# Three PSUM slots and three one-hot buffers in the two attention passes of a graph network, in place of two each

## What is computed

```
h       = (x @ W).reshape(N, heads, outc)
alpha_s = (h * a_s).sum(-1);  alpha_d = (h * a_d).sum(-1)
e     = leaky_relu(alpha_s[src] + alpha_d[dst], 0.2)
m     = segment_max(e, dst);  p = exp(e - m[dst])
z     = segment_sum(p, dst);  alpha = p / (z[dst] + 1e-16)
out   = segment_sum(h[src] * alpha[:, :, None], dst)
```

## Time and profile before

| | us |
|---|---|
| median of 3 runs | 25891.91 |
| lowest and highest | 25857.63, 25914.94 |
| profiled execution: span | 25860.5 |
| PE busy | 20502.8 |
| DVE busy | 19538.6 |
| POOL busy | 14550.5 |
| ACT busy | 12983.1 |
| first attention pass, first to last start of its fetch matmuls | 861.1 to 3825.1 |
| second attention pass, likewise | 4282.1 to 8128.3 |

### The profile page before, as it was taken

One profiled execution on the slowest core, in us unless ns is written; L12 is line 12 of the kernel. 1 busy time (PEld: TensorE's weight loads), 2 busy tenths in 40 slices (PEclk: granted clock), 3 DMA queues, 4 the chain that ended last, 5 costly groups with the idle time before them and its releaser, 6 DMA issues. The chain is left out here.

```text
span 25860.5 us, 355868 instructions
## 1 busy us (share of the span) xinstructions
PE 20502.8 (79%) x110397; PEld 18592.4 (72%) x110397; DVE 19538.6 (76%) x36629; ACT 12983.1 (50%) x15054; POOL 14550.5 (56%) x14357
## 2 busy tenths in 40 slices
PE   0688874888885799978999638888888889489996
PEld 0577763888785688867888538888888888278885
DVE  4699995777776699987999626666666667499997
ACT  0455551222221466644666316666666667266664
POOL 1555545555554555554555467666776675355555
PEclk9999996999997899998999859999999999599998
DMA  5222221111111111111111111111111111522221
GB/s 91 59 71 71 71 69 22 37 40 37 40 37 31 37 40 40 40 32 40 36 35 35 23 14 19 19 19 18 19 18 19 19 19 15 147 67 71 71 71 50
DMA packets 1347467, 1106.63 MB, mean 43 GB/s; under 512 B 937658, under 2 KB 1197972, under 8 KB 1320180
## 3 DMA queue, kind: packets, MB, share of 16 engines
q1 hardware_dynamic: 673364, 571.63, 8.0%
q0 software_dynamic: 545440, 167.01, 7.8%
q10 hardware_dynamic: 127872, 358.35, 3.8%
HBM read 646.52 MB, written 448.94 MB: 42 GB/s over the span
## 5 line engine op out<-in xcount | busy, mean ns | idle before, releaser
L973 PE MATMUL gat_e_found<-gat_e_parts,gat_e_lowhot 128*128 128x400 f32 x27776 | 5657.0, 363 | 1270.4 <-DVE gat_e_rows L937 974.6
L973 PEld LDWEIGHTS gat_e_found<-gat_e_parts,gat_e_lowhot 128*128 128x128 f32 x27776 | 5301.1, 199 | 1625.9 <-DVE gat_e_rows L937 1225.8
L1091 POOL DMA_INDIRECT gat_e_rows<-att_t,gat_e_index x3968 | 3767.0, 949 | 3046.1 <-issue 1509.8
L1966 PEld LDWEIGHTS rgcn_e_found<-rgcn_e_parts,rgcn_e_lowhot 128*128 128x128 f32 x23808 | 4295.3, 188 | 667.9 <-DVE rgcn_e_picked L1811 455.5
L760 POOL DMA_INDIRECT rgcn_e_rows<-rel_t,rgcn_e_index x3472 | 3284.4, 946 | 2506.3 <-DMA rgcn_e_rows<-rel_t,rgcn_e_index 1137.9
L1966 PE MATMUL rgcn_e_found<-rgcn_e_parts,rgcn_e_lowhot 128*128 128x400 f32 x23808 | 4543.8, 348 | 173.4 <-DVE rgcn_e_picked L1811 133.8
L2527 PE MATMUL sheaf_e_bysrc<-sheaf_e_exacthot,sheaf_e_masked 128*128 128x392 f32 x19840 | 4217.8, 370 | 423.7 <-ACT sheaf_e_exacthot L2630 365.4
L2258 POOL DMA_INDIRECT sheaf_e_rows<-sheaf_t,sheaf_e_index x3224 | 3386.3, 1050 | 1695.5 <-issue 886.8
L2527 PEld LDWEIGHTS sheaf_e_bysrc<-sheaf_e_exacthot,sheaf_e_masked 128*128 128x128 f32 x19840 | 3844.2, 206 | 533.1 <-ACT sheaf_e_exacthot L2630 400.0
L2630 ACT CAST sheaf_e_exacthot<-sheaf_e_eighthhot 128x1568 fp32r<-128x1568 bf16 x2480 | 3587.9, 1501 | 919.9 <-DVE sheaf_e_eighthhot L2341 549.4
L973 PE MATMUL typed_e_found<-typed_e_parts,typed_e_lowhot 128*128 128x400 f32 x11904 | 2372.3, 351 | 338.0 <-DVE typed_e_hrows L937 242.1
(11 more groups left out here) (515 smaller groups left out, 27971.4 us busy)
## 6 DMA issues: line engine op xcount, KB each, us to landing
rgcn_e_low<-few_low_d SPq DMA_DIRECT2D x124, 768.0 KB
typed_e_types<-in_type_t SPq DMA_DIRECT2D x62, 1536.0 KB
sumsatt<-gat_e_sums ACTq DMA_DIRECT2D x62, 1404.0 KB
typed_t<-typed_p_y SPq DMA_DIRECT2D x98, 765.0 KB
sumsatt<-gat_e_sums ACTq DMA_DIRECT2D x62, 1092.0 KB
gat_e_rows<-att_t,gat_e_index POOLq DMA_INDIRECT x3968
rgcn_e_rows<-rel_t,rgcn_e_index POOLq DMA_INDIRECT x3472
sumsrel<-rgcn_e_sums ACTq DMA_DIRECT2D x124, 416.0 KB
```

Source lines behind the costliest of these rows:

```text
L973: last = pe.matmul(self.found_ps[n % 2][:, c + b, 0:w], hot[:, k, col * P:(col + 1) * P], self.table.column(part, k)[:, b * w:(b + 1) * w] ...
L1091: pool.indirect_dma_start(rows_t[a.k][:, j, :], None, table, rows(index[a.k][:, j:j + 1]))\
L1966: last = pe.matmul(found_ps[c // 2][:, c % 2, 0:FHI * FD], low_hot[at % 2][:, n, c * P:(c + 1) * P], short.column(part, n), start=n == 0 a ...
```

## The change

`Finder` gets a number of slots, 2 by default, and the attention passes ask for 3. There are three PSUM slots of two banks, and three `low_hot` tiles. They are used in rotation within a turn of two chunks, and the rotation starts anew with each turn. In the first pass a turn has 24 halves and 12 groups, which three divides; in the second it has 32 halves and 8 groups, and there the method `reuse` works out at the first two places of a turn that the buffer was last used only two halves (groups) ago, and keeps the wait as it was.

```
-        self.low_hot = [s.sb(f"lowhot{k}", [P, cut.tiles, QC * P], cut.exact) for k in range(2)]
+        self.low_hot = [s.sb(f"lowhot{n}", [P, cut.tiles, QC * P], cut.exact) for n in range(slots)]
...
-        self.found_ps = [s.ps(f"found{k}", [P, 2, 256 if size <= 256 else 512]) for k in range(2)]
+        self.found_ps = [s.ps(f"found{n}", [P, 2, 256 if size <= 256 else 512]) for n in range(slots)]
...
+    def hot_of(self, a, q):
+        return self.low_hot[(a.k * self.groups + q) % self.slots]
+    def found_of(self, a, n):
+        return self.found_ps[(a.k * self.halves + n) % self.slots]
+    def reuse(self, a, at, per):
+        if a.k == 1 or a.is_first() or at >= self.slots:
+            return self.slots
+        return min(self.slots, at + 1 + (2 * per - 1 - at) % self.slots)
...
     def find(self, pe, a, n, first=False):
-        if not (first and n < 2):
-            pe.wait_ge(self.taken, H - 1)
-        hot = self.low_hot[(a.k * self.groups + n // self.per_group) % 2]
+        if not (first and n < self.slots):
+            pe.wait_ge(self.taken, H + 1 - self.reuse(a, n, self.halves))
+        hot = self.hot_of(a, n // self.per_group)
...
     def build_low(self, act, a, q, fresh=False):
-        if not (fresh and q < 2):
-            act.wait_ge(self.found, self.per_group * (G - 1))
-        act.activation(self.low_hot[(a.k * self.groups + q) % 2][:, :, :], self.away[:, :, :], ACT.Relu, bias=1.0,
+        if not (fresh and q < self.slots):
+            act.wait_ge(self.found, self.per_group * (G + 1 - self.reuse(a, q, self.groups)))
+        act.activation(self.hot_of(a, q)[:, :, :], self.away[:, :, :], ACT.Relu, bias=1.0,
...
-        f = HelpedFinder(s, g, quarters(g, even=found_w % 4 != 0), sources, found_w, columns)
+        f = HelpedFinder(s, g, quarters(g, even=found_w % 4 != 0), sources, found_w, columns, slots=3)
```

More of the change, by code:

```diff
@@ L863, with __init__ @@
 class Finder:
-    def __init__(self, s, g, cut, sources, width, columns, rest=None):
-        self.g, self.cut, self.width, self.columns = g, cut, width, columns
+    def __init__(self, s, g, cut, sources, width, columns, rest=None, slots=2):
+        self.g, self.cut, self.width, self.columns, self.slots = g, cut, width, columns, slots
         size = width * cut.highs
@@ L906, in build_low @@
             dve.wait_ge(self.found, self.per_group * (a.c * self.groups + q - 1))
-        hot = self.low_hot[(a.k * self.groups + q) % 2]
+        hot = self.hot_of(a, q)
         for n in range(self.cut.tiles):
@@ L930, in take @@
         o.link(dve.tensor_tensor(self.picked[:, :, :, :],
-                                 self.found_ps[n % 2][:, :, 0:w * highs].rearrange("p c (f h) -> p c f h", f=w),
+                                 self.found_of(a, n)[:, :, 0:w * highs].rearrange("p c (f h) -> p c f h", f=w),
                                  high, ALU.mult))
@@ L972, in find @@
                     for b in range(self.banks):
-                        last = pe.matmul(self.found_ps[n % 2][:, c + b, 0:w],
+                        last = pe.matmul(self.found_of(a, n)[:, c + b, 0:w],
                                          hot[:, k, col * P:(col + 1) * P],
@@ L981, with __init__ @@
 class HelpedFinder(Finder):
-    def __init__(self, s, g, cut, sources, width, columns, rest=None):
-        super().__init__(s, g, cut, sources, width, columns, rest)
+    def __init__(self, s, g, cut, sources, width, columns, rest=None, slots=2):
+        super().__init__(s, g, cut, sources, width, columns, rest, slots)
         self.away = s.sb("away", [P, cut.tiles, QC * P], F16)
```

## The result

| | median us | lowest to highest | ratio to before |
|---|---|---|---|
| before (10 runs, same chip) | 25882.64 | 25846.54 to 25914.94 | |
| changed (10 runs) | 25752.39 | 25607.12 to 25860.62 | 0.9944, 95% interval 0.9924 to 0.9964 |

The change makes the kernel 0.56% faster where 2.5% was forecast. Its executions spread over 1.0%, those of the kernel before over 0.26%. The profiled one is among its shortest: its time is 25623.17 us, its span 25621.4. In the other experiments the kernel before takes 25,853 to 26,193 us (medians), so kernels of different experiments are compared by their ratio to it.

What follows compares the result with a forecast made beforehand. In both attention passes PE and DVE were taken to wait for each other for too few buffers. 25860.5 - 577 (second pass) - 68 (first) = 25215 us profiled; 31 more gives the median, 25,247. Range 25,070 to 25,660.

Steps and rivals of the forecast that it cites:

- any wait of DVE for a product can be shorter by PE's time for a half, 3.0 us: Second pass: a third slot lets PE hold one more half, so waits under 3.0 us can vanish.
- I take 30%, 4.0 us: Second pass: of DVE's 13.3 us of product waits a chunk 4.0 stay, giving 52.7 us a chunk, gain 577 us.
- the late signal: Second pass: a finished product is signalled late to DVE, costing DVE 4.2 us and PE 3.4 us in one case.
- (a): Rival, both passes: late signal not caught up, hitting every fourth half instead of every third; gain 236 us, 25,656; chance 0.22.
- (d): Rival, slower: signal held back until PE stops, waits 5.1 us instead of 2.07; plus 694 us, 26,590; chance 0.04.
- point of decision: Second-pass mean DVE wait of 2.8 us, beyond which the kernel gets slower if signals wait until PE stops.
- (b): Rival, both passes: DVE's waits go entirely and POOL binds at 50.7 and 46.0 us; gain 812 us, 25,080; chance 0.13.
- (c): Rival: no change, 25,890, because what PE and DVE wait for is decided elsewhere; chance 0.06.
- The first pass: First attention pass: 47.8 us a chunk falls to 46.7, near POOL's 46.6; gain 68 us, bounds 0 to 112.
- The own paces: Second pass, each engine's time a chunk without waits for others: DVE 48.7 us, POOL 50.7, PE 47.9.
- The one-hot tile: Third tile takes nothing from PE in the second pass, is needed in the first; its effect was put at zero.
- The rule weighed in the prediction: PE idling briefly while cycling PSUM banks keeps falling to the lower clock; second-pass clock would stay at 0.94 with three slots.

Runs made afterwards that it cites:

- e1: Changed kernel with three PSUM slots but only two one-hot tiles; 0.9959 of the kernel before.
- e4: Changed kernel with a second-pass half's matmuls done one PSUM bank after the other, not in turns; 0.9946 of the kernel before.
- e7: Changed kernel with zeros for node values in the table PE multiplies with in both attention passes; 0.9957 of the kernel before.
- e15: Kernel before (two slots) with a POOL pause after every 6 second-pass gathers instead of 9; 0.9858 of the kernel before.
- e13: Changed kernel (three slots) with a POOL pause after every 6 second-pass gathers instead of 9; 0.9797 of the kernel before.
- e9: Changed kernel (three slots) with 32 of 36 row gathers a chunk left out in the second pass; 0.9602 of the kernel before.
- e10: Kernel before (two slots) with 32 of 36 row gathers a chunk left out in the second pass; 0.9658 of the kernel before.
- e12: Changed kernel with a POOL pause after every 18 second-pass gathers instead of 9; 1.045 of the kernel before.
- e16: Changed kernel (three slots) with a POOL pause after every 8 second-pass gathers instead of 9; 0.9835 of the kernel before.
- e11: Changed kernel with a POOL pause after every 4 second-pass gathers instead of 9; 0.9933 of the kernel before.
- e3: Kernel before with three slots and tiles in the first pass only; 0.9976 of the kernel before.
- e17: Changed kernel with each second-pass row gather fetching 8 floats a row instead of 34; 0.9898 of the kernel before.
- e2: Kernel before with two PSUM slots but three one-hot tiles; 1.0026 of the kernel before.

## Why the prediction was wrong

**The step that failed** is "any wait of DVE for a product can be shorter by PE's time for a half, 3.0 us", and with it "I take 30%, 4.0 us". Of DVE's 13.3 us of waits a chunk it left 4.0; the same sum of rows after is 533 of 3000 us, 10.4 us a chunk, and that in one of its shortest executions. So the chunk takes 58.5 us in the profile and not 52.7, and by the median, with 68 us for the whole second pass, some 61. The prediction took the late signal for a delay of fixed length that a deeper buffer covers. The records show one that grows with the buffer: 3.7 us late with two slots, and with three 6.4 us in the changed kernel's profile and 8.1 to 8.7 in e1, e4 and e7. With a pause every 6 gathers it is 3.2 and 7.8 us (e15, e13). With two slots PE had run all of its next half and stopped in 167 of 262 late products before DVE got its signal; with three it runs on for 25 matmuls on average (16 is a half) in place of 14, and then its matmuls come in steps of 0.70 us. What the third slot took from PE's waits between halves, 5.5 us a chunk, came back in part inside the halves (2.0 us in the profiled execution, 4.8 to 6 in e1, e4 and e7).

**What makes the products late** is POOL's unbroken run of row gathers. That is shown: without them (e9, e10) DVE's waits go, with longer runs and as many gathers (e12) they grow to 35.9 us a chunk, with shorter ones (e16, e13, e15) the pass gets faster until POOL's pauses bind it (e11). A pause lets the outstanding transfers land, so a long run also means many transfers outstanding; these two are not told apart. The prediction had POOL as an engine with a pace of its own only, and wrote "I cannot say from the trace what delays the signal"; the profile of before had the lead in it, since most of the delays end in POOL's pauses.

**The worth of the slot.** The prediction gave nearly all of DVE's 13.3 us a chunk to the missing slot. e10 shows what it is: with two slots and no run of gathers DVE is idle 1.7 us a chunk before its multiplies, where it was 14.4, and the pass takes 49.5 against 48.1 with three. So nearly all of the wait was POOL's. The slot is worth 0.6% in each setting: 0.9944 beside 1, 0.9602 / 0.9658 = 0.9942, and 0.9797 / 0.9858 = 0.9938. That is both passes together; the first gives 0.24% of it (e3).

**The rivals.** (a) had the number of the profiled execution (58.7 forecast, 58.5 found), but that was luck: there are as many late products as before, not three quarters, each is later, and the median, 25,752, lies 96 us above its 25,656. (d) was right that the signal comes later with one more slot, but not in its condition, that it is held back until PE stops: PE had filled its slots ahead of the signal in 167 of 262 cases before and had run the 31 or 32 matmuls that it could in only 21 of 261 after. Nor was it right in the price: DVE's waits went to 533 us, not up. Its point of decision, a mean wait of 2.8 us, was not reached: 533 / 224 = 2.4 us, against 2.07 before. (b) fell: POOL still waits 329.9 us for `rows_used`. (c) fell as a number, in the second pass narrowly (0.9976 with the slot in the first pass alone, 0.9944 with it in both), but its reason, that what PE and DVE wait for is decided elsewhere, is what e10 shows of the second pass.

**What held.** The first pass: 46.7 forecast, 46.5 found, 68 us against 62 to 82. The own paces: DVE's 48.7 and PE's 47.9 stand against the 48.1 us that e9 takes, POOL's 50.7 plus 1.94 us for each of two more pauses is 54.6 against the 56.4 of e13, in experiments where the kernel before takes 1.1 to 1.2% longer. The one-hot tile at zero: e1 and the whole change can't be told apart.

**The clock.** The granted clock of 4800 to 7800 went from 0.94 to 0.95, and of 992 halves 61 in place of 124 ran for the most part at 0.50. Of the 262 late products of before, 261 ended at a clock of 1.00, so the clock is not what makes them late. The rule weighed in the prediction (the Trainium skill, "TensorE: Matmul & The Clock Gate", section "A second HAM failure mode: psum-queue depth-cycling") would have kept the clock where it was; the stretch's mean agrees, the count of halves does not. In e9, where PE hardly stops, and in e10 the clock of 4800 to 7200 is 1.00.

**What stays open.** What in a gather holds PE back. e17 rules out the bytes as the main cause; the work that POOL does to issue it and the 128 small transfers of each are not told apart. The Trainium skill, "Perfetto Trace Analysis", section "DMA Instruction — SWDGE (GPSIMD)", says that POOL's span of such an instruction is the writing of its descriptors and not the moving of data. The trace agrees: the span is 0.94 us with 34 floats a row and 0.95 with 8. Nor is it known why the relational passes, with as many matmuls a half and a pause of POOL every 6 gathers, show little of it: by the same count the first has 16 late products in 744 and 3 gaps, at PE busy 97%, the second 95, 2.3 us late, and no gap. Open too is why e2 is slower, and why kernels with three slots differ so much from one execution to the next.

## To carry to other kernels

Before buying a deeper buffer against a wait, ask whether the wait ends with the producer's work or with something else: here the product had, by the records, been finished for 3.7 us, and the delay grew with the buffer that was to cover it. Look at what every other engine, not only the two that wait, does when a late signal arrives. If GpSimd issues many indirect DMAs, the number between two of its pauses is a setting to be measured: 4, 6, 8, 9 and 18 gave 0.9933, 0.9797, 0.9835, 0.9944 and 1.045 here.

## What was not expected of the hardware

- A run of indirect DMAs on GpSimd (1.25 us each) slows TensorE, which reads nothing of theirs: matmuls of 0.19 us then start mostly at multiples of about 0.70 us, at a granted clock of 1.00 (two thirds of the changed kernel's gaps) as of 0.50. The longest stretch of this in the changed kernel, pauses of POOL included, is 35 us; without the gathers (e9) there is none.
- What the records show as the end of a matmul can lie 20.8 us ahead of the start of the DVE instruction that waits for it (mean of e12's late products).
- A pause of GpSimd costs 1.94 us (2.24 us between two gathers in place of 0.30), and behind it TensorE took 11 and 9 matmuls at once in the timeline above.
- Three one-hot tiles in place of two, with two PSUM slots, cost 0.26% (e2, 1.0016 to 1.0035), unexplained.
